# A Graph and Attention Layer with a Routed Feed-Forward Net on One Core: Token Search, Placing and the Net's First Lists Rewritten

## The chip, the cores and the metric

The kernel runs on one core of a Trainium2 chip. The metric is the device time of one execution in microseconds, start to end. The profile is one execution, and all its times are counted from the start of its span. The engines are named as the profile names them: PE is TensorE, DVE VectorE, ACT ScalarE, POOL GpSimd, SP SyncE.

## The reference

The input is 12,500 rows of 256 floats with 200,000 edges sorted by destination. Three things are added up, and a routed net follows:

```
xn = layernorm(x)
x = x + graph(xn) + attention_block(xn)
#   graph: relu(mean over edges of xn[src] @ W_l.T + b_l + xn @ W_r.T) + xn
#   attention_block: linear attention with elu+1, its norm, an MLP, its norm, residual
x = x + routed(layernorm(x))

def routed(x):                          # 12500 rows
    weights = x @ wr + br               # one number per row
    _, idx = top_k(weights, 6250)
    sel = idx[:6249]                    # KK = 6249 rows
    y = gelu(x[sel] @ w1 + b1) @ w2 + b2    # 256 -> 1024 -> 256
    y = y * weights[sel]
    return zeros.at[sel].set(y) + x
```

The change concerns how the 6249 rows are chosen and brought to the routed net. The graph and attention stages compute the same with the same instructions.

## The kernel before, in words

Rows are held as 98 blocks (NBLK) of 128; row number = block x 128 + lane. A [128, 98] tile has one entry per row of the input. The work runs in stages, and each engine has one instruction list, written out by hand, with semaphores between the engines; an engine does its list in order, so the order in the source is the order in time. `own.link(x)` makes the engine that issued x wait until x is done before its next instruction.

1. Layer norm, gathers of source rows (POOL, L708), one-hot segment sums on PE, attention and MLP. None of it is changed.
2. **The graph product stage**: 49 steps of two blocks. POOL loads `lin_raw` (L722), PE turns the means (L1535) and multiplies (L1718, L1722), DVE adds and takes statistics (L1076 to L1102), ACT scales (L1440), SP stores rows to `out_rows` (L636). Ahead of it DVE's list has the reciprocals of the counts (L1058), the sum of `wr` (L1059) and the small tables of the search (L1061 to L1069). Its first job in the stage itself is L1076, which waits for PE's first product.
3. **The search** (DVE L1128 to L1181, PE L1736 to L1743). DVE makes a sortable integer of each row's weight, splits it into two halves of 16 bits held as float32, and finds the KK-th largest in eight rounds of one digit of four bits, four rounds for the high half and four for the low one. In a round DVE compares all 98 entries with 15 candidates (L1152, in two parts of 4 and 3 chunks of 14 blocks: 840 and 630 results per lane, the candidate running fastest in the result `s_ge`, float16). PE sums each of the seven chunks over lanes into PSUM by a product with a tile of ones (L1741), DVE adds over blocks (L1159), counts the candidates that still have KK rows (L1161) and forms the next candidates (L1164, L1166). Behind the first comparisons of all DVE also writes the coefficients of the layer norm for the net (L1139 to L1142), which SP stores to `coef_d` (L653).
4. **The ranks** (DVE L1180 to L1202, PE L1745 to L1756): ties, and for every chosen row its place in the list of 6249, as a column (0 to 48) and a lane.
5. **The placing** (DVE L1203 to L1213, ACT L1466 to L1470, PE L1757 to L1763): for each of seven chunks of 14 blocks DVE compares the columns (`s_is`, 14 x 49 results, L1207) and the lanes (`s_oh`, 14 x 128, L1209) and multiplies `s_is` by the block number (`s_pc`'s second half, L1212); ACT multiplies `s_is` by the lane (`s_pc`'s first half, L1470). PE then takes 14 products of `s_oh` (the weights) with `s_pc` (L1761). Two buffers of each alternate; from the third chunk on DVE and ACT wait until PE is done with the chunk two before. All arrays are float16 with the entry 0..48 or 0..127 running fastest.
6. **The net** (25 steps of up to 256 rows). DVE writes the row lists (L1217 to L1220). POOL copies a step's list (L731) and issues two gathers of rows (L743) and two of coefficients (L746), step by step. Float32 products are made of rounded parts and what is left: ACT rounds the weights (L1474, L1475), DVE subtracts (`fw1_l` L1224, `fw2_l` L1225), norms a step's rows (L1237), PE turns them (L1774), ACT rounds them (L1481), DVE subtracts (L1231), and PE multiplies (L1782), 48 matmuls with `w1` and 48 with `w2` in a step. PE waits once, ahead of the first step, until both subtractions of the weights are done (`f_wl`).

The two loops around which the change is made are these:

```
for h in range(2):                                        # L1149
    o, w = PCH * sum(CHALF[:h]), PCH * CHALF[h]
    v.tensor_tensor(s_ge[:, o:o + w, :], keys[:, o:o + w].unsqueeze(2)...,   # float32
                    bcast(s_cand, w, CAND), ALU.is_ge).then_inc(s_cnt, 1)
...
e.wait_ge(f_wh, 2)                                        # L1223
v.tensor_tensor(fw1_l, fw1_s, fw1_h.bitcast(f32), ALU.subtract).then_inc(f_wl, 1)
v.tensor_tensor(fw2_l, fw2_s, fw2_h.bitcast(f32), ALU.subtract).then_inc(f_wl, 1)
```

Of the kernel before, what the change touches and what calls it, by code (L numbers as in the profile page):

```python
# [13 lines left out]
P = 128  # L14
# [26 lines left out]
HALFD = 16 // DIGIT  # L41
NDIG = 2 * HALFD
# [3 lines left out]
CHALF = (NPCH - NPCH // 2, NPCH // 2)  # L46
# [69 lines left out]
def build(nc, x, src, dst, W_l, b_l, W_r, Wq, Wk, Wv, Wm, W1, W2, g1, b1, g2, b2, wr, br, w1, fb1, w2, fb2, out):  # L116
# [13 lines left out]
    with ctx:  # L130
# [221 lines left out]
        f_in = [sem(f"f_in{i}") for i in range(FSLOTS)]  # L352
        f_T_ps = sem("f_T_ps")
# [68 lines left out]
        s_tab = part(topk, 0, (HALFD, 16))[:, :, 0:CAND]  # L422
        s_unit = part(topk, 64, (HALFD, 16))[:, :, 0:CAND]
        s_cand, s_next, s_counts, s_got = (topk[:, a:a + CAND] for a in (128, 144, 160, 176))
        s_found, s_prefix, s_left, s_above = (topk[:, a:a + 1] for a in (192, 193, 194, 195))
        s_key, s_half = (topk[:, a:a + NBLK].bitcast(i32) for a in (300, 400))
        s_hi, s_low, s_over, s_keys = (topk[:, a:a + NBLK] for a in (500, 600, 700, 800))
# [3 lines left out]
        iota16, tri16, ones16 = (topk16[:, a:a + P] for a in (0, 128, 256))  # L431
        col16, blk16 = topk16[:, 384:384 + NSEL], topk16[:, 448:448 + NBLK]
# [4 lines left out]
        s_ge = work[:, 6144:6144 + NBLK * CAND // 2].bitcast(f16).rearrange("p (b k) -> p b k", k=CAND)  # L437
        s_oh, s_is, s_pc = ([work[:, a + w * k:a + w * k + PCH * m // 2].bitcast(f16).rearrange("p (b m) -> p b m", b=PCH)
# [220 lines left out]
        def _(e):  # L659
# [73 lines left out]
            def f_io(i, s, j):  # L733
# [8 lines left out]
                for u in range(n):  # L742
# [22 lines left out]
        def _(e):  # L765
# [302 lines left out]
            v.tensor_scalar(col16, iotaf[:, 0:NSEL], -64.0, None, ALU.add)  # L1068
# [65 lines left out]
            own.link(v.tensor_copy(s_hi, s_half))
            v.tensor_copy(s_low, s_key)

            def coefficients():

                v.tensor_copy(gcoef[:, :, 0], gmv[:, :, 0])  # L1139
                v.tensor_copy(gcoef[:, :, 2], wtok[:, :])  # L1140
                own.link(v.reciprocal(gve, gg))
                v.tensor_tensor(gcoef[:, :, 1], gf, gve, ALU.mult).then_inc(coef_set, 1)  # L1142

            def search(keys, first):

                v.memset(s_prefix, 0.0)
                own.link(v.tensor_copy(s_cand, s_tab[:, 0, :]))
                for r in range(HALFD):
                    n = first + r  # L1149
                    for h in range(2):  # L1150
                        o, w = PCH * sum(CHALF[:h]), PCH * CHALF[h]
                        v.tensor_tensor(s_ge[:, o:o + w, :], keys[:, o:o + w].unsqueeze(2).to_broadcast([P, w, CAND]),  # L1152
                                        bcast(s_cand, w, CAND), ALU.is_ge).then_inc(s_cnt, 1)
                    if r + 1 < HALFD:
                        v.tensor_scalar(s_next, s_tab[:, r + 1, :], s_prefix, None, ALU.add)
                    if n == 0:
                        coefficients()
                    e.wait_ge(s_tot, n + 1)
                    own.link(v.tensor_reduce(s_counts, part(ps[:, BA, :], 0, (PCH, CAND)).rearrange("p b k -> p k b"),  # L1159
                                             AX.X, ALU.add))  # L1160
                    own.link(v.tensor_scalar(s_got, s_counts, float(KK), None, ALU.is_ge, ALU.add,  # L1161
                                             accum_out=s_found))
                    if r + 1 < HALFD:
                        own.link(v.scalar_tensor_tensor(out=s_cand, in0=s_unit[:, r, :], scalar=s_found, in1=s_next,  # L1164
                                                        op0=ALU.mult, op1=ALU.add))
                    own.link(v.scalar_tensor_tensor(out=s_prefix, in0=s_unit[:, r, 0:1], scalar=s_found, in1=s_prefix,  # L1166
                                                    op0=ALU.mult, op1=ALU.add))
# [337 lines left out]
        def _(e):  # L1505
# [281 lines left out]
            def f_body(i, s, j):  # L1787
# [16 lines left out]
                if past(i, 1):  # L1804
                    e.wait_ge(f_yb, i)
# [35 lines left out]
```

## Time and profile before

| What | us |
|---|---|
| Median of 3 runs (2602.32 to 2604.92) | 2603.88 |
| The profiled execution's own time | 2605.66 |
| Its span, first to last instruction | 2603.9 |
| PE busy in the span | 2193.5 (84%) |
| DVE busy in the span | 1329.9 (51%) |
| POOL busy in the span | 1695.5 (65%) |
| PE's mean granted clock, as a share of 2.4 GHz | 0.934 |

Of a row of the profile: `L1209 DVE TENSOR_TENSOR work<-srcI 128x1792 f16` is an instruction of line 1209 on DVE which writes the tile `work` from `srcI`, 128 lanes of 1792 results. In a timeline, a row begins with the start and the duration in us; brackets hold the time that the engine stood idle before it and what ended that. In a table by stage, each engine has its busy time and its number of instructions. Durations of DVE instructions include a start and an end that overlap the neighbour, so that two which follow each other with no wait start closer together than the first one's duration.

### The profile page before, as it was taken

How to read it: one execution, taken by the hardware profiler on the slowest of the kernel's cores; microseconds unless marked ns; L12 is line 12 of the kernel's file. 1: busy time of each engine (PE TensorE's matmuls, PEld its weight loads, DVE VectorE, ACT ScalarE, POOL GpSimd, SP SyncE). 2: the span in 40 equal slices, each digit the busy share in tenths (PEclk: the TensorE clock that was granted, in tenths of full speed). 3: DMA queues.
4: the chain of work that ended last, by engine and by line, in shares of the span. 5: the costliest groups of instructions: out<-in, count | busy, mean ns of one | idle time of the engine just before them, and what ended most of it. 6: DMA issues, size and time to landing. Idle time of an engine off the chain costs nothing.

```text
span 2603.9 us, 48868 instructions
## 1 busy us (share of the span) xinstructions
PE 2193.5 (84%) x13352; PEld 1818.9 (70%) x13353; DVE 1329.9 (51%) x3157; ACT 901.4 (35%) x1949; POOL 1695.5 (65%) x1817
## 2 busy tenths in 40 slices
PE   1399999997888888888888888988899799379998
PEld 0287777775667666666676666777677688279998
DVE  8644444443444344454444454455555599844444
ACT  8433333331222222222222222222222268344554
POOL 3577777777777777777777777777777411045553
PEclk7699999998898999999999999999999899589999
DMA  9766666654555555555555555555555489611111
GB/s 326 232 194 186 184 184 179 188 181 146 160 157 153 152 154 164 157 160 155 153 158 160 153 161 157 152 153 165 158 162 166 142 276 297 214 34 43 45 44 35
DMA packets 218373, 419.29 MB, mean 161 GB/s; under 512 B 40580, under 2 KB 107142, under 8 KB 218287
## 3 DMA queue, kind: packets, MB, share of 16 engines
q0 software_dynamic: 88352, 243.57, 33.0%
q1 hardware_dynamic: 129118, 173.95, 19.9%
q8 instruction: 34, 0.56, 0.1%
q10 hardware_dynamic: 816, 0.79, 0.1%
q14 instruction: 53, 0.43, 0.1%
HBM read 321.63 MB, written 96.52 MB: 161 GB/s over the span
## 4 chain that ended last, share of the span: by engine, by line
PE 45%; POOL 29%; issue 13%; DVE 7%; DMA 5%; ACT 1%; DVEq 1%; POOLq 0%; ACTq 0%
POOL gath_raw L708 28%; PE ps L1782 11%; PE ps L1629 6%; PE ps L1550 5%; PE ps L1552 4%; PE ps L1595 4%; DMA gath_raw<-xtab,srcI 3%; PE ps L1722 3%; PE ps L1639 3%; PE ps L1535 2%; PE ps L1677 2%; PE ps L1647 1%; DVE stats L784 1%; PE ps L1609 1%; DVE gath_raw L803 1%
## 5 line engine op out<-in xcount | busy, mean ns | idle before, releaser
L708 POOL DMA_INDIRECT gath_raw<-xtab,srcI x1563 | 1483.6, 949 | 476.5 <-issue 460.7
L1550 PE MATMUL ps<-gath_raw,onehot 128*128 128x256 f16 x1956 | 480.3, 283 | 202.8 <-DMA gath_raw<-xtab,srcI 107.6
L880 DVE SCALAR_TENSOR_TENSOR onehot<-ps,blkbase,dstF 128x512 f32 x489 | 353.9, 745 | 257.8 <-issue 154.5
L1552 PE MATMUL ps<-gath_raw,onehot 128*128 128x257 f16 x1956 | 481.5, 283 | 0.0
L1550 PEld LDWEIGHTS ps<-gath_raw,onehot 128*128 x1956 | 195.2, 100 | 292.9 <-issue 263.4
L1629 PE MATMUL ps<-work,w_s 128*128 128x256 f32 x1568 | 392.9, 407 | 2.2 <-issue 1.7
L1629 PEld LDWEIGHTS ps<-work,w_s 128*128 128x128 f32 x1568 | 311.7, 204 | 48.7 <-issue 2.7
L954 DVE BATCH_NORM_STATS2 stats<-ps 128x6 f32<-128x256 f32 x196 | 74.4, 421 | 449.2 <-PE ps L1677 444.6
L1782 PE MATMUL ps<-split_raw 128*128 128x256 f32 x2376 | 293.3, 285 | 1.7 <-DVE split_raw L1231 1.5
L1782 PEld LDWEIGHTS ps<-split_raw 128*128 128x128 f32 x2376 | 288.4, 193 | 2.4 <-issue 1.9
L1363 ACT ACTIVATE work<-ps 128x512 f32<-128x512 f32 x98 | 58.5, 597 | 496.8 <-PE ps L1629 496.8
L1552 PEld LDWEIGHTS ps<-gath_raw,onehot 128*128 x1956 | 197.2, 101 | 40.3
L1595 PE MATMUL ps<-wkv_s,work 128*128 128x256 f32 x784 | 183.1, 387 | 5.4 <-issue 4.7
L1639 PE MATMUL ps<-w_s,work 128*128 128x256 f32 x784 | 182.3, 385 | 0.0
L1595 PEld LDWEIGHTS ps<-wkv_s,work 128*128 128x128 f32 x784 | 146.1, 191 | 25.3 <-issue 5.4
L1639 PEld LDWEIGHTS ps<-w_s,work 128*128 128x128 f32 x784 | 144.9, 190 | 18.5
L1398 ACT ACTIVATE work<-ps,b_s,g_s 128x256 f32<-128x256 f32 x98 | 49.9, 560 | 247.3 <-PE ps L1535 247.3
L1368 ACT ACTIVATE small<-small 128x2 f32<-128x2 f32 x98 | 19.9, 203 | 329.6 <-DVE small L962 329.6
L1495 ACT ACTIVATE agg<-ps,fb_s 128x256 f32<-128x256 f32 x200 | 83.9, 470 | 138.4 <-PE ps L1782 138.4
L1535 PE MATMUL ps<-ident,work 128*128 128x128 f32 x784 | 124.6, 282 | 5.6 <-ACT work L1422 5.6
L722 POOL DMA_DIRECT2D lin_raw<-lin_d x49 | 26.0, 532 | 124.6 <-PE ps L1722 109.0
L1535 PEld LDWEIGHTS ps<-ident,work 128*128 128x128 f32 x784 | 91.1, 142 | 17.8 <-ACT work L1422 5.7
(223 smaller groups left out, 2989.9 us busy)
## 6 DMA issues: line engine op xcount, KB each, us to landing
work<-x_in SPq DMA_DIRECT2D x98, 256.0 KB, 3.2
lin_raw<-lin_d POOLq DMA_DIRECT2D x49, 512.0 KB, 4.4
gath_raw<-xtab,srcI POOLq DMA_INDIRECT x1563
agg<-x_in SPq DMA_DIRECT2D x14, 896.0 KB, 7.4
xt_d<-work SPq DMA_DIRECT2D x49, 256.0 KB
q_d<-work SPq DMA_DIRECT2D x49, 256.0 KB, 2.7
work<-q_d SPq DMA_DIRECT2D x49, 256.0 KB, 3.4
work<-xt_d SPq DMA_DIRECT2D x49, 256.0 KB, 3.1
```

Source lines behind the costliest of these rows:

```text
L708: e.indirect_dma_start(out=gath[:, TPG * s + t, 0:2 * D], out_offset=None, in_=xtab[:, :], in_offset=bass.IndirectOffsetOnAxis(ap=srcI[:, ...
L880: v.scalar_tensor_tensor(out=onehots[:, ds(p % OHN * TPG, TPG), :], in0=ps[:, columns:columns + 1, 0:P].to_broadcast(shape), scalar=blkbas ...
L954: last = v.bn_stats(ln_st[k][:, u, :], src[:, u, :])
L1495: last = a.activation(fh[:, c, :], bank(BB + h)[:, c % 2, :], ACT.Gelu_apprx_tanh, bias=fb1_s[:, c:c + 1])
L1535: last = t.transpose(bank(b)[:, c, u * P:(u + 1) * P], of[:, u, c * P:(c + 1) * P], ident[:, :])
L1550: t.matmul(ps[:, ds(BG + k % 2, 1), 0:D], oh, gath[:, r, 0:D], start=False, stop=False, skip_group_check=True)
L1552: last = t.matmul(ps[:, ds(BG + k % 2, 1), 0:AGW], oh, gath[:, r, D:2 * D + 1], start=False, stop=q == TPG - 1, skip_group_check=True)
L1595: last = t.matmul(bank(BC + b)[:, u, :], kxT[s][:, c, u * P:(u + 1) * P], wkv_s[:, c, b * D:(b + 1) * D], start=c == 0, stop=c == 1)
L1629: last = t.matmul(bank(BD + h)[:, o_ % 2, :], w1_s[:, c, o_ * P:(o_ + 1) * P], (mxT[s] if c < 2 else mynT)[:, c % 2, :], start=c == 0, sto ...
L1639: last = t.matmul(bank(BF)[:, u, :], mh1[:, c, u * P:(u + 1) * P], w2_s[:, c, :], start=c == 0, stop=c == 3)
L1722: last = t.matmul(to[:, u, :], gaT[i % 2][:, c, u * P:(u + 1) * P], wlT[:, c, :], start=False, stop=c == 1, skip_group_check=True)
L1782: last = t.matmul(to, left[l], right[r], start=start and k == 0, stop=stop and k == 2)
```

## The change

- **Digits as tokens.** Eight digits of four bits are read straight from the 32-bit key (a shift and a mask into `s_nib`, then a cast with 1 added), each kept as float16 1 to 16. One search of eight rounds replaces two of four. The fixed candidates 2 to 16 stand in a table laid out over blocks (`cand_rep`), and instead of new candidates each round ends with a new token: the next digit where the entry is equal to what was found, 32 where it is above, 0 where below (three DVE operations).
- **Layout.** `s_ge`, `s_oh`, `s_is` and `s_pc` are transposed inside a lane: the block runs fastest, and the candidate, the lane or the column is the slower one. The constants they are compared with are spread into tables beforehand (`cand_rep` 15 x 98, `lane_rep` 128 x 14, `col_rep` 49 x 14), in the space of the gathered rows, behind a wait for the last group. Everything compared is float16. PE's weights and moving data of L1761 are then columns with a step of 14 elements (28 bytes); in the search its moving data are 15 runs of 14.
- **Halves.** The first comparison of a round covers 3 chunks, the second 4 (it was 4 and 3).
- **Coefficients.** The four instructions behind the first round are spread over the first four rounds.
- **The net's start.** POOL signals `f_sent` when it has issued the gathers of step 0; DVE waits for that before it subtracts `fw1_l`, and subtracts `fw2_l` behind step 0's own norm and subtraction. PE waits for `fw1_l` ahead of step 0's first product and for `fw2_l` ahead of its second.

```diff
-CHALF = (NPCH - NPCH // 2, NPCH // 2)
+CHALF = (NPCH // 2, NPCH - NPCH // 2)
...
+        s_dig = [topk16[:, 1920 + 112 * r:1920 + 112 * r + NBLK] for r in range(NDIG)]
+        rep16 = gath_raw[:, 0:2048].bitcast(f16)
+        cand_rep = part(rep16, 0, (CAND, NBLK))
+        lane_rep = part(rep16, 1472, (P, PCH))
+        col_rep = part(rep16, 3264, (NSEL, PCH))
...
-        s_ge = work[:, 6144:6144 + NBLK * CAND // 2].bitcast(f16).rearrange("p (b k) -> p b k", k=CAND)
+        s_ge = work[:, 6144:6144 + NBLK * CAND // 2].bitcast(f16).rearrange("p (k b) -> p k b", k=CAND)
...
+                if not past(i, 1):
+                    e.sem_inc(f_sent, 1)
...
-            for r in range(HALFD):
-                step = float(1 << (16 - DIGIT * (r + 1)))
-                v.tensor_scalar(s_tab[:, r, :], iotaf[:, 1:CAND + 1], step, None, ALU.mult)
-                v.memset(s_unit[:, r, :], step)
-            v.tensor_copy(iota16, iotaf[:, :])
+            e.wait_ge(grp_used, NG)
+            v.tensor_copy(cand_rep, spread(iotaf[:, 2:CAND + 2], CAND, NBLK))
+            v.tensor_copy(lane_rep, spread(iotaf[:, 0:P], P, PCH))
+            v.tensor_scalar(col_rep, spread(iotaf[:, 0:NSEL], NSEL, PCH), -64.0, None, ALU.add)
+            v.memset(s_counts[:, CAND:CAND + 1], 3.0e38)
...
+            def digit(r):
+                own.link(v.tensor_scalar(s_nib, s_key, 32 - DIGIT * (r + 1), CAND, ALU.logical_shift_right, ALU.bitwise_and))
+                own.link(v.tensor_scalar(s_dig[r], s_nib, 1.0, None, ALU.add))
+            digit(0)
+            token = s_dig[0]
+            for r in range(NDIG):
+                for h in range(2):
+                    b = slice(PCH * sum(CHALF[:h]), PCH * sum(CHALF[:h + 1]))
+                    v.tensor_tensor(s_ge[:, :, b], over(token[:, b], CAND), cand_rep[:, :, b], ALU.is_ge).then_inc(s_cnt, 1)
+                if r + 1 < NDIG:
+                    digit(r + 1)
...
+                if r == 2:
+                    own.link(v.reciprocal(gve, gg))
...
+                e.wait_ge(s_tot, r + 1)
+                own.link(v.tensor_reduce(s_counts[:, 0:CAND], part(ps[:, BA, :], 0, (CAND, PCH)), AX.X, ALU.add))
+                own.link(v.tensor_scalar(s_got, s_counts, float(KK), None, ALU.is_ge, ALU.add, accum_out=s_found))
+                if r + 1 < NDIG:
+                    v.scalar_tensor_tensor(out=s_among, in0=token, scalar=s_found, in1=s_dig[r + 1],
+                                           op0=ALU.is_equal, op1=ALU.mult)
+                    own.link(v.tensor_scalar(s_above_at, token, s_found, 2.0 * (CAND + 1), ALU.is_gt, ALU.mult))
+                    token = s_next[r % 2]
+                    own.link(v.tensor_tensor(token, s_among, s_above_at, ALU.add))
...
+                v.tensor_tensor(s_is[k], col_rep, over(s_col[:, b], NSEL), ALU.is_equal).then_inc(s_in_col, 1)
+                v.tensor_tensor(s_oh[k], lane_rep, over(s_pos[:, b], P), ALU.is_equal)
...
+                v.tensor_tensor(s_pc[k][:, NSEL:2 * NSEL, :], s_is[k], over(blk16[:, b], NSEL), ALU.mult).then_inc(s_a, 1)
...
-            e.wait_ge(f_wh, 2)
+            e.wait_ge(f_sent, 1)
+            e.wait_ge(f_wh, 1)
             v.tensor_tensor(fw1_l, fw1_s, fw1_h.bitcast(f32), ALU.subtract).then_inc(f_wl, 1)
-            v.tensor_tensor(fw2_l, fw2_s, fw2_h.bitcast(f32), ALU.subtract).then_inc(f_wl, 1)
...
             f_norm(0, 0, 0)
             f_low_x(0, 0)
+            e.wait_ge(f_wh, 2)
+            v.tensor_tensor(fw2_l, fw2_s, fw2_h.bitcast(f32), ALU.subtract).then_inc(f_wl, 1)
...
-                    last = t.matmul(ps[:, BD, 0:2 * NSEL], s_oh[c % 2][:, k, :], s_pc[c % 2][:, k, :],
+                    last = t.matmul(ps[:, BD, 0:2 * NSEL], s_oh[c % 2][:, :, k], s_pc[c % 2][:, :, k],
...
-            e.wait_ge(f_wl, 2)
+            e.wait_ge(f_wl, 1)
...
+                else:
+                    e.wait_ge(f_wl, 2)
```

## Rows read from the trace of the kernel before

**Rows 1.** The page's shares by engine and line of the chain that ended last

```profile
PE 45%; POOL 29%; issue 13%; DVE 7%; DMA 5%; ACT 1%; DVEq 1%; POOLq 0%; ACTq 0%
```

**Rows 2.** Stages: window, length, busy us (PE, PEld, DVE, ACT, POOL), clock, DMA share, GB/s

```profile
2220.50:2253.10 32.60, 11.42 (x56) 5.73 (x56) 26.26 (x79) 15.80 (x33) 0.00 (x0) 0.50 1.01 341
2258.00:2284.00 26.00, 9.28 (x98) 7.77 (x98) 24.60 (x21) 9.38 (x9) 0.00 (x0) 0.50 0.00 1
2298.80:2603.90 305.10, 297.73 (x2470) 297.18 (x2470) 139.44 (x245) 154.55 (x325) 145.97 (x163) 0.99 0.14 42
```

**Rows 3.** Groups by shape, DVE: count, busy us, mean ns, idle before

```profile
L1119 DVE TENSOR_TENSOR gath_raw<-gath_raw 128x98 f32<-128x98 f32 x1 | 0.3, 261 | 0.0
L1193 DVE TENSOR_TENSOR srcI<-srcI 128x98 f16<-128x98 f16 x1 | 0.2, 211 | 0.0
```

**Rows 4.** Timeline of one round of the search (the second), to the next round's first row

```profile
2226.42 1.76 DVE L1152 TENSOR_TENSOR work<-dstF 128x840 f16<-128x840 f32 x2
2228.23 0.31 PEld L1741 LDWEIGHTS ps<-work,srcI 128*128 128x128 f16 x3 [0.25 <-DVE work L1152]
2228.97 0.38 DVE L1159 TENSOR_REDUCE dstF<-ps 128x15 f32<-128x210 f32 x1 [0.66 <-PE ps L1741]
2229.60 0.23 DVE L1164 SCALAR_TENSOR_TENSOR dstF<-dstF 128x15 f32<-128x15 f32 x1
2230.12 1.76 DVE L1152 TENSOR_TENSOR work<-dstF 128x840 f16<-128x840 f32 x2
```

**Rows 5.** Timeline, DVE: where the search begins and ends, and three operations in it

```profile
2220.52 0.21 DVE L1128 TENSOR_SCALAR dstF<-wtok 128x98 f32<-128x98 f32 x1
2221.31 0.21 DVE L1132 TENSOR_SCALAR dstF<-dstF 128x98 int32<-128x98 int32 x1
2224.31 0.76 DVE L1141 RECIPROCAL gath_raw<-gath_raw 128x98 f32<-128x98 f32 x1
2237.70 0.32 DVE L1173 SCALAR_TENSOR_TENSOR dstF<-dstF 128x98 f32<-128x98 f32 x1
2253.12 0.32 DVE L1180 TENSOR_SCALAR_CACHE_REDUCE srcI<-dstF 128x98 f16<-128x98 f32 x1
```

**Rows 6.** Timeline of the placing's last chunk and what follows it

```profile
2279.02 0.86 DVE L1207 TENSOR_TENSOR work<-srcI 128x686 f16<-128x686 f16 x1
2279.80 2.02 DVE L1209 TENSOR_TENSOR work<-srcI 128x1792 f16<-128x1792 f16 x1
2281.74 0.86 DVE L1212 TENSOR_TENSOR work<-work,srcI 128x686 f16<-128x686 f16 x1
2282.66 1.32 PE L1761 MATMUL ps<-work 128*128 128x98 f16 x14 [2.17 <-DVE work L1212]
2284.02 0.21 DVE L1217 TENSOR_SCALAR dstF<-ps 128x49 f32<-128x49 f32 x1 [1.42 <-PE ps L1761]
```

**Rows 7.** Timeline from the row lists to the net's first products

```profile
2284.74 2.28 DVE L1224 TENSOR_TENSOR split_raw<-agg,split_raw 128x2048 fp32r<-128x2048 f32 x1
2284.89 2.18 POOL L731 COPY agg<-agg 128x4 int32<-128x4 int32 x1 [78.17 <-DVE agg L1220]
2287.91 2.25 POOL L743 DMA_INDIRECT agg<-out_rows,agg  x1 [0.83 <-POOL agg L731]
2293.00 0.94 POOL L746 DMA_INDIRECT agg<-coef_d,agg  x1 [0.30 <-issue]
2293.94 0.20 POOL L731 COPY agg<-agg 128x4 int32<-128x4 int32 x1
2294.96 0.96 POOL L743 DMA_INDIRECT agg<-out_rows,agg  x1 [0.81 <-POOL agg L731]
2295.35 0.73 DVE L1237 TENSOR_SCALAR agg<-agg 128x256 f32<-128x256 f32 x2 [6.12 <-DMA agg<-coef_d,agg]
2298.82 8.04 PE L1782 MATMUL ps<-split_raw 128*128 128x256 f32 x48 [1.50 <-DVE split_raw L1231]
```

**Rows 8.** Timeline, DVE: the first addition of the graph product stage

```profile
2085.48 0.69 DVE L1076 SCALAR_TENSOR_TENSOR agg<-ps,work 128x512 f32<-128x512 f32 x1 [5.91 <-PE ps L1722]
```

More of the change, by code:

```diff
@@ L421, in build @@
         topk = dstF[:, :, :].rearrange("p g t -> p (g t)")
[L422 to L427, printed above, removed]
+        s_counts, s_got = (topk[:, a:a + CAND + 1] for a in (160, 176))
+        s_found, s_left, s_above = (topk[:, a:a + 1] for a in (192, 194, 195))
+        s_key, s_sign, s_nib = (topk[:, a:a + NBLK].bitcast(i32) for a in (300, 400, 500))
+        s_bits = topk[:, 800:800 + NBLK]
         s_rk, s_rcol, s_rpos = (topk[:, a:a + NBLK].bitcast(i32) for a in (900, 1000, 1100))
@@ L1134, in _ @@
[L1134 to L1167, printed above, removed]
@@ L1177, in _ @@
-            search(s_keys, HALFD)
-            v.tensor_scalar(s_gt, s_keys, s_prefix, None, ALU.is_gt, ALU.add, accum_out=s_above)
-            v.tensor_scalar(s_eq, s_keys, s_prefix, None, ALU.is_equal).then_inc(s_cnt, 1)
+            own.link(v.tensor_scalar(s_bits, wtok[:, :], 0.0, None, ALU.add))
+            bits = s_bits.bitcast(i32)
+            own.link(v.tensor_scalar(s_sign, bits, 31, -(1 << 31), ALU.arith_shift_right, ALU.bitwise_or))
+            own.link(v.tensor_tensor(s_key, bits, s_sign, ALU.bitwise_xor))
@@ new lines, in digit, with over @@
+            def digit(r):
+                own.link(v.tensor_scalar(s_nib, s_key, 32 - DIGIT * (r + 1), CAND, ALU.logical_shift_right, ALU.bitwise_and))
+                own.link(v.tensor_scalar(s_dig[r], s_nib, 1.0, None, ALU.add))
+            def over(ap, n):
+                return ap.unsqueeze(1).to_broadcast([P, n, ap.shape[1]])
+            digit(0)
[6 more added lines that the diff above has]
+                    digit(r + 1)
+                if r == 0:
+                    v.tensor_copy(gcoef[:, :, 0], gmv[:, :, 0])
+                if r == 1:
+                    v.tensor_copy(gcoef[:, :, 2], wtok[:, :])
+                if r == 2:
+                    own.link(v.reciprocal(gve, gg))
+                if r == 3:
+                    v.tensor_tensor(gcoef[:, :, 1], gf, gve, ALU.mult).then_inc(coef_set, 1)
+                e.wait_ge(s_tot, r + 1)
[7 more added lines that the diff above has]
+                    own.link(v.tensor_tensor(token, s_among, s_above_at, ALU.add))
@@ L1183, in ranked @@
+            v.tensor_scalar(s_gt, token, s_found, None, ALU.is_gt, ALU.add, accum_out=s_above)
+            v.tensor_scalar(s_eq, token, s_found, None, ALU.is_equal).then_inc(s_cnt, 1)
             def ranked(n):
@@ L1469, in _ @@
                     e.wait_ge(s_mm, c - 1)
-                a.activation(s_pc[c % 2][:, :, 0:NSEL], s_is[c % 2], ACT.Copy, scale=pcol[:, 0:1]).then_inc(s_lane, 1)
+                a.activation(s_pc[c % 2][:, 0:NSEL, :], s_is[c % 2], ACT.Copy, scale=pcol[:, 0:1]).then_inc(s_lane, 1)
             e.wait_ge(ffw_in, 32)
@@ L1740, in _ @@
                         e.wait_ge(s_cnt, 2 * r + 1 + (c > 0))
-                    last = t.matmul(ps[:, BA, 0:PCH * CAND], ones16, flat(s_ge[:, c * PCH:(c + 1) * PCH, :]),
+                    last = t.matmul(part(ps[:, BA, :], 0, (CAND, PCH)), ones16, s_ge[:, :, c * PCH:(c + 1) * PCH],
                                     start=c == 0, stop=c == NPCH - 1)
```

34 lines of the change are left out of this document (9 added, 25 removed).

## The prediction

> **What bounds the kernel now.** I read the page's chain first: PE holds 45% of it, POOL 29% and DVE only 7% [rows 1]. So DVE looks like a side matter, and over the whole span it is. The table by stage says where it is not. For 32.60 us of the search DVE is busy 26.26, and for 26.00 us of the placing it is busy 24.60, while PE has 11.42 and 9.28 and sits at half its clock (0.50, 1.2 GHz). Behind them lies the net, where PE is busy 297.73 of 305.10 us: whatever is saved ahead of it moves the net forward whole [rows 2]. The third place is the gap between the row lists and the net's first product, in which POOL's issues are the chain [rows 7]. These three stretches, some 73 us, are all that the change can win from.
>
> **Comparing at float16, block fastest (the large term).** The comparisons of the placing run at one result per cycle of 0.96 GHz: starts are 0.78 us apart for 686 results, 1.94 for 1792, 0.78 for the multiplication, 3.50 a chunk [rows 6]. That is 1.0417 ns a result and 0.066 us an instruction. Their data are float16 already, but one operand repeats the same element along the fastest direction. What would they cost with both operands running? One pair of rows of equal length answers: 98 results took 261 ns in float32 and 211 ns in float16 with all three operands plain [rows 3]. The 50 ns between them are 98 x 0.52 ns, half a cycle each. So I take 0.5208 ns a result. A chunk becomes (686 + 1792 + 686) x 0.5208 ns + 3 x 0.066 = 1.65 + 0.20 = 1.85 us. Seven chunks save 7 x (3.50 - 1.85) = **11.6 us**. ACT's product of a chunk starts behind the first comparison; even if all of ACT's 9.38 us in the placing [rows 2] were these seven, one would be 1.34, less than the 1.43 that DVE's other two then take.
>
> PE's side of a chunk is 1.32 us for 14 matmuls [rows 6], at half clock. It fits in 1.85 as long as a matmul stays under 1.85 / 14 = 0.13 us. After the change weights and moving data are read with a step of 28 bytes, and no row shows a matmul reading so. From below the cost is nothing (98 columns at 1.2 GHz are 0.082 us, 14 of them 1.14 of the 1.32, so there is no gain to be had); from above nothing in the trace bounds it, and I carry it as a rival. I take none, because the half clock leaves every column twice the time it has at full clock.
>
> The Trainium skill speaks against this (SBUF — State Buffer, section Door 1: The DMA port swizzle, on cachelines): SBUF has lines of 16 bytes, and a read that goes to a new line each time pays a penalty, so that float16 may be stepped by 8 elements for free, and the change steps by 14. The page gives no price; by its rule PE could need twice the time, and the sum would be that of the first rival below. No row of this trace shows it.
>
> **The search.** A round is now 3.70 us [rows 4]. Step by step:
> - The two comparisons, 1470 results: 1.76 becomes 630 x 0.5208 + 0.066 for the first and 840 x 0.5208 + 0.154 (start and end) for the second, 0.985 us.
> - From their end to the reduction: PE's last group took 2228.97 - 2228.18 = 0.79 with three matmuls. It now has four, each 210 columns at 1.2 GHz, 0.175: 0.965.
> - Reduction and count: 2229.60 - 2228.97 = 0.63, unchanged.
> - The new candidates took 0.52 (2229.60 to 2230.12). The token takes three operations: a SCALAR_TENSOR_TENSOR of 98 (0.32 long, 0.24 to the next start, since nothing waits) [rows 5], a waited-for TENSOR_SCALAR (0.25 and 0.035) and a TENSOR_TENSOR (0.21 and 0.035) [rows 3]: 0.77.
>
> A round is 3.35, the last 2.58 without the token. The next digit's two waited-for operations (0.25 each) lie in PE's 0.97 us, as does a copy in rounds 0 and 1. In round 2 the reciprocal of 0.76 [rows 5] comes on top: 0.5 + 0.8 exceeds the cover by some 0.25 us. Ahead of the rounds five waited-for operations take the place of eight: three of them span 0.79 (2220.52 to 2221.31) [rows 5], five 1.28. Between the halves nothing is left. In all 1.28 + 7 x 3.35 + 0.25 + 2.58 = 27.56 us, against 2253.12 - 2220.52 = 32.60 [rows 5]: **5.0 us**. Its parts: comparisons 8 x 0.775 = 6.2 saved, PE's fourth matmul 8 x 0.175 = 1.4 given back, the token 7 x 0.25 = 1.75 given back, ends and middle 2.0 saved.
>
> **The net's start.** Both subtractions begin beside POOL's first copy, each 2.28 us. The copy took 2.18 us where the next one took 0.20, and the first gather 2.25 where a later one took 0.96 [rows 7]; nothing else differs, so the subtractions hold POOL up. Without them POOL's last issue of step 0 ends 1.98 + 1.3 = 3.3 us earlier, 5.8 us behind the lists instead of 9.1, and its data would reach DVE at 7.2 (L746's start to L1237 is 2.35) instead of 10.5. But DVE now begins `fw1_l` at 5.8 and ends it at 8.15, and L1237 is behind it in DVE's list. What is late next is thus the subtraction: **2.35 us** saved, 3.3 the bound if it cost nothing, and 1.4 if POOL's next copy or gather gets ahead of it. Who else waits: POOL's issues for step 1 are held up by `fw1_l` and perhaps by `fw2_l` (2 x 2.2 us), so step 1's rows are there at about 17.5 us behind the lists; PE asks for them when its first 48 matmuls, 8.04 us long [rows 7], are over, at 11.6 + 8.0 = 19.6. `fw2_l` ends at 14, far ahead of that. Cost nothing, slack 2 us.
>
> **The tables.** `cand_rep`, `lane_rep`, `col_rep` are 3948 results, 4.1 us at one per cycle, some 3.2 us more than what they replace. DVE stands idle 5.91 us before L1076 [rows 8]: hidden even at one per cycle. Without that cover it would be 3.2 us. The wait for the last group is over by then. **Transfers**: the lists are now due near 2268; the DMA share is 0.00 from 2258.00 on [rows 2], so stores, weights and coefficients have landed.
>
> **The sum** is 5.0 + 11.6 + 2.35 = 19.0 us. The profiled execution took 2605.66 us (span 2603.9), so it would take 2586.7. The median of the runs, 2603.88, is 1.8 below it: **2584.9 us**.
>
> **The rivals.**
> 1. PE's stepped reads bind the placing, mildly: each matmul twice 0.082. A chunk is 14 x 0.163 = 2.3 us; the placing is 7 x 0.45 = 3.1 us longer and the last chunk's tail 1.1. That gives 2589.1, still faster. For it: no row shows such a read. Chance 0.12.
> 2. The new comparisons don't run at two per cycle (a repeated outer direction or runs of 14 spoil it). Then the placing saves nothing, the search is 6.2 - 5.0 = 1.2 us longer than now, the lists save 2.35: 2602.7, no change. For it: the one float16 row is a single plain run of 98 [rows 3]. Against: the fastest direction is now as in that row, and runs of 15 cost nothing extra at one per cycle (1470 results in 1.76) [rows 4]. Chance 0.08.
> 3. Slower: stepped reads at a price that makes PE the bound of the placing. It decides from where 98 matmuls outlast what is saved: to lose 0.2% (5.2 us), the placing must take 26.0 + 5.0 + 2.35 + 5.2 = 38.6 us instead of 26.0, less 2.0 at its ends 36.6, or 0.37 us a matmul, 4.6 times now. At six times (0.49) it is 98 x 0.49 + 2 = 50 us, and the time 2603.9 + 24 - 7.35 = 2620.6. Against: no row shows a matmul that slow. Chance 0.04.
> 4. The lists' gain fails (POOL's next issue gets ahead of `fw1_l`, step 1 late): 1 to 3 us back, 2587. It is inside the range. Chance 0.06.
>
> **The numbers.** The forecast has 0.70. What two runs of this kernel can be told apart by is 0.2%, 5.2 us. Faster takes the forecast, rivals 1 and 4: 0.88; no change is rival 2, 0.08; slower is rival 3, 0.04. Downward the range adds the lists' bound of 3.3 instead of 2.35 (0.95), a cheaper token and a run's scatter of 1.3: 2581.5. Upward it takes in rivals 1 and 4: 2591.
>
> **What would show it.** In the profile after: L1209's successor near 1.08 us for 1792 results and chunks 1.85 us apart, with PE's 14 matmuls still 1.3; rounds 3.35 us apart; POOL's first copy 0.2 us; the first net product about 11.6 us behind the row lists instead of 14. Wrong would be: 2.0 us for 1792 results (rival 2); DVE idle before a chunk's first comparison, ended by PE (rivals 1, 3); the first addition of the graph product stage later than now.

## The result, and the profile after

| | before | after |
|---|---|---|
| Median of six runs, us | 2604.4 | 2592.99 |
| Ratio, 95% interval | | 0.9955 (0.9941 to 0.9968) |
| Span of the profiled execution, us | 2603.9 | 2589.7 |
| Search, first key operation to L1180 / L1178 | 32.6 | 28.0 |
| Ranks | 4.9 | 4.9 |
| Placing, first comparison to the row lists' first operation | 26.0 | 20.0 |
| End of the row lists to the net's first product | 14.0 | 12.85 |
| First product to the end | 305.1 | 304.9 |

The kernel became 11.4 us faster, with the interval 8.3 to 15.4 (0.0032 to 0.0059 of 2604.4). Forecast were 19.0, and the measured time lies 2.0 us above the range. One of the six executions of the changed kernel was slow, 5558.56 us; the ratio leaves it out, and without it the median would be 2592.84. The three stretches give 4.6 + 6.0 + 1.15 = 11.75 us, so the trace accounts for the measured gain. The two profiled spans differ by 14.2, but 2.3 of these lie ahead of the search, where none of the three terms of the forecast lies: its first operation starts at 2218.25 instead of 2220.52.

The table by stage of the changed kernel, beside [rows 2] (window, length, busy time of PE, PEld, DVE, ACT and POOL with counts, granted clock, DMA share, GB/s):

```profile
2218.20:2246.30 28.10, 11.22 (x56) 5.89 (x56) 22.38 (x86) 15.84 (x33) 0.00 (x0) 0.50 1.02 345
2251.10:2271.20 20.10, 18.01 (x98) 13.84 (x98) 13.56 (x22) 9.68 (x9) 0.00 (x0) 0.50 0.00 1
2284.80:2589.70 304.90, 297.44 (x2470) 296.90 (x2470) 141.53 (x246) 154.67 (x325) 147.53 (x163) 0.99 0.14 42
```

The second row is where the expected gain went. In the placing DVE's busy time fell from 24.60 us to 13.56, as meant, but PE's rose from 9.28 to 18.01 of 20.10 us, on the same 98 products at the same clock. The stage has a new bound.

A chunk of the placing, as a timeline (start, duration; in brackets the idle time before and what ended it), beside [rows 6]:

```profile
2253.13 18.01 PE L1758 MATMUL ps<-work 128*128 128x98 f16 x98 [3.06 <-DVE work L1208]
2263.54 0.52 DVE L1205 TENSOR_TENSOR work<-gath_raw,srcI 128x686 f16<-128x686 f16 x1 [0.60 <-PE ps L1758]
2263.97 1.09 DVE L1206 TENSOR_TENSOR work<-gath_raw,srcI 128x1792 f16<-128x1792 f16 x1
2264.97 0.51 DVE L1208 TENSOR_TENSOR work<-work,srcI 128x686 f16<-128x686 f16 x1
2266.08 0.52 DVE L1205 TENSOR_TENSOR work<-gath_raw,srcI 128x686 f16<-128x686 f16 x1 [0.60 <-PE ps L1758]
2271.17 0.21 DVE L1212 TENSOR_SCALAR dstF<-ps 128x49 f32<-128x49 f32 x1 [3.14 <-PE ps L1758]
```

The comparisons run at two results per cycle: 1792 in 1.08 to 1.09 us where it was 2.02, 686 in 0.52 where it was 0.86. But PE, once started, has one unbroken run of 98 matmuls, and DVE stands 0.60 us ahead of a chunk until PE gives a buffer back. Chunks start 2266.08 - 2263.54 = 2.54 us apart, not 1.85. And the last chunk ends with 3.14 us of waiting where it was 1.42. This is what the prediction named as the sign of rival 1.

A round of the search, beside [rows 4]:

```profile
2233.31 0.99 DVE L1156 TENSOR_TENSOR work<-srcI,gath_raw 128x630 f16<-128x630 f16 x2
2233.85 1.41 PE L1738 MATMUL ps<-work,srcI 128*128 128x210 f16 x7 [1.97 <-DVE work L1156]
2234.46 0.21 DVE L1146 TENSOR_SCALAR srcI<-dstF 128x98 f16<-128x98 int32 x1
2235.36 0.38 DVE L1168 TENSOR_REDUCE dstF<-ps 128x15 f32<-128x210 f32 x1 [0.69 <-PE ps L1738]
2235.99 0.32 DVE L1171 SCALAR_TENSOR_TENSOR srcI<-srcI,dstF 128x98 f16<-128x98 f16 x1
2236.75 0.99 DVE L1156 TENSOR_TENSOR work<-srcI,gath_raw 128x630 f16<-128x630 f16 x2
```

The comparisons take 0.99, the token 2236.75 - 2235.99 = 0.76, and the next digit's operations (L1146 is the second) are hidden beside PE. Only PE's part is longer than worked out: 1.06 us from the end of the comparisons to the reduction, not 0.965. A round is 3.44. PE's seven matmuls are one run of 1.41 us, where it was 1.43: moving data in runs of 14 elements cost PE nothing here.

The start of the net, beside [rows 7]; the row lists end at 2271.99 (L1215, 2271.78 and 0.21 long):

```profile
2272.05 0.19 POOL L736 COPY agg<-agg 128x4 int32<-128x4 int32 x1 [67.67 <-DVE agg L1215]
2273.06 1.05 POOL L748 DMA_INDIRECT agg<-out_rows,agg  x1 [0.83 <-POOL agg L736]
2274.28 2.29 DVE L1220 TENSOR_TENSOR split_raw<-agg,split_raw 128x2048 fp32r<-128x2048 f32 x1 [2.30 <-POOLq L755]
2274.42 3.02 POOL L751 DMA_INDIRECT agg<-coef_d,agg  x1 [0.30 <-issue]
...
2281.37 0.73 DVE L1232 TENSOR_SCALAR agg<-agg 128x256 f32<-128x256 f32 x2 [4.79 <-DMA agg<-coef_d,agg]
2284.84 7.68 PE L1779 MATMUL ps<-split_raw 128*128 128x256 f32 x48 [1.50 <-DVE split_raw L1226]
```

The copy is short now (0.19, it was 2.18), but the stall has only moved: the second gather takes 3.02 us, where the third and fourth take 0.95 and 0.94. The subtraction was let go at 2274.28 by "POOLq L755", the queue's signal written behind all four gathers, when one of the four had run. The norm (L1232) still waits for its data, 4.79 us after the subtraction.

The tables, made ahead of the graph product stage (DVE's timeline), beside [rows 8]:

```profile
2077.36 1.67 DVE L1073 CAST gath_raw<-iotaf 128x1470 f16<-128x1470 f32 x1
2078.94 1.08 DVE L1074 CAST gath_raw<-iotaf 128x1792 f16<-128x1792 f32 x1
2079.94 0.86 DVE L1075 TENSOR_SCALAR gath_raw<-iotaf 128x686 f16<-128x686 f32 x1
2084.31 0.69 DVE L1086 SCALAR_TENSOR_TENSOR agg<-ps,work 128x512 f32<-128x512 f32 x1 [3.10 <-PE ps L1719]
```

Of 5.91 us of idle time 3.10 are left: the tables are hidden, as forecast.

### The profile page after: what moved, and what is told of

It is laid out like the page before. It is cut to its first block, busy times and chain, and to the rows that moved or that the text cites. A ratio compares the mean times of both kernels' runs of the same rounds, so it can differ in the third digit from the quotient of the medians.

```text
span 2589.7 us, 48874 instructions
## 1 busy us (share of the span) xinstructions
PE 2200.0 (85%) x13352; PEld 1826.8 (71%) x13353; DVE 1316.4 (51%) x3156; ACT 902.0 (35%) x1949; POOL 1696.3 (66%) x1817
## 4 chain that ended last, share of the span: by engine, by line
POOL 37%; PE 37%; issue 14%; DVE 5%; DMA 4%; ACT 1%; DVEq 1%; POOLq 0%; SPq 0%; ACTq 0%
POOL gath_raw L713 37%; PE ps L1779 11%; PE ps L1626 4%; PE ps L1547 3%; PE ps L1719 3%; PE ps L1549 3%; PE ps L1592 3%; DMA gath_raw<-xtab,srcI 3%; PE ps L1636 2%; PE ps L1532 2%; DVE stats L791 1%; PE ps L1674 1%; PE ps L1644 1%; DVE gath_raw L810 1%; PE ps L1715 1%
```

## The experiments

The chips of these runs were slower than the first one: the kernel before took 3063.6 us (median of 25 runs) beside the first four, 3109.2 beside the next four (one run) and 3095.9 (18 runs) beside the last four. Nearly all of that lies ahead of the search: in the changed kernel run again (e11), the first addition of the graph product stage comes at 2568.7 us instead of 2084.3, which is 484 of the 495 us by which its span is longer. The search took 28.0 us in every one of these runs and the placing 20.0 wherever it was unchanged, as on the first chip. Repeats of one kernel scatter by 8 to 24 us there, so the verdicts below rest on the stretches, each read from one profile; the ratios are given beside them. The next four, e5 to e8, ran once each, 3091.1, 3094.2, 3101.4 and 3078.5 us beside 3109.2, and no verdict rests on these times: e6, whose placing is 8 us longer than before the change, would come out 15 us faster.

**e1: the placing undone.**

```diff
-                v.tensor_tensor(s_oh[k], lane_rep, over(s_pos[:, b], P), ALU.is_equal)
+                v.tensor_tensor(s_oh[k], bcast(iota16, PCH, P), s_pos[:, b].unsqueeze(2).to_broadcast([P, PCH, P]),
+                                ALU.is_equal)
...
-                    last = t.matmul(ps[:, BD, 0:2 * NSEL], s_oh[c % 2][:, :, k], s_pc[c % 2][:, :, k],
+                    last = t.matmul(ps[:, BD, 0:2 * NSEL], s_oh[c % 2][:, k, :], s_pc[c % 2][:, k, :],
...
```

The comparison of the columns and both products are turned back in the same way.

> The changed kernel with the placing as it was before (entry running fastest, comparisons at one result per cycle). Theory A (the stepped reads make PE the bound of the placing, so the new layout saves 6.0 us there and not 11.6): the placing takes 26.0 us again instead of 20.0, a chunk 3.50, PE's 14 matmuls 1.32 us a chunk; time 2593.0 + 6.0 = 2599.0. Theory B (the layout gave its 11.6 and the loss lies outside the three stretches): 2604.6.

Placing 26.0 us, as in theory A. The ratio to the kernel before, 0.9990 (0.9972 to 1.0008), holds theory A's time (0.9979) and theory B's (1.0001), so it is the stretch that decides. PE's matmuls, by the view of one line (minimum, median and maximum ns), are back at their old length:

```profile
L1761 PE MATMUL ps<-work x98: 260/282/285, 2705.5 to 2727.6; 128*128 128x98 f16 x98
```

**e2: the net's start undone.**

```diff
-            e.wait_ge(f_sent, 1)
-            e.wait_ge(f_wh, 1)
+            e.wait_ge(f_wh, 2)
             v.tensor_tensor(fw1_l, fw1_s, fw1_h.bitcast(f32), ALU.subtract).then_inc(f_wl, 1)
+            v.tensor_tensor(fw2_l, fw2_s, fw2_h.bitcast(f32), ALU.subtract).then_inc(f_wl, 1)
...
```

The signal, the later `fw2_l` and PE's two separate waits go too.

> The changed kernel with both subtractions of the net's weights ahead of the first lists again. Theory A (the signal leaves POOL too early, so that part is worth 1.15 us and not 2.35): from the last instruction of the row lists to the net's first product 14.0 us instead of 12.85; time 2594.2. Theory B (that part gave its 2.35): 2595.4, the difference in the stretch 2.35. Theory C (it gave nothing): 2593.0 and the stretch unchanged.

From the start of the lists' last instruction to the first product: 14.2 us, against 13.1 in the changed kernel on these chips (e7, e11) and 13.0 on the first. That is 1.1 to 1.2, theory A (whose 14.0 and 12.85 count from that instruction's end, 0.2 later). The same stretch is 13.0 to 13.4 in the versions that change the placing alone (e1, e5, e6, e8), so it is good to some 0.3 us: enough against B's 2.35 and C's nothing. The ratio, 0.9974 (0.9962 to 0.9985), doesn't tell the theories apart: their times are 0.9956 to 0.9965.

**e3: the search alone.** The edits of e1 and e2 together.

> Only the search of the change, with the placing and the net's start of before. Theory A (the search is worth what its stretch shows, 4.6 us, and the parts add up): 2604.4 - 4.6 = 2599.8, search 28.0 us, placing 26.0, row lists to first product 14.0. Theory B (the parts don't add up, what is saved in one is given back in the next): over 2602.

Search 28.0, placing 26.0, and 14.5 us from the start of the lists' last instruction to the first product (14.2 in the kernel before and in e2). The ratio, 0.9991 (0.9970 to 1.0012), holds both theories' times (0.9982 and over 0.9991). Each part is thus seen to be independent of the others by its stretch; that the whole time adds up was not resolved.

**e4: wait for POOL's copy instead of the signal.**

```diff
-                if not past(i, 1):
-                    e.sem_inc(f_sent, 1)
...
-            e.wait_ge(f_sent, 1)
+            e.wait_ge(fstage[1], 1)
```

> The changed kernel in which DVE waits, ahead of its first subtraction, for POOL's copy of the second step's list instead of the signal that POOL's instruction list raises behind the four gathers of the first. Theory A (the signal is raised when the gathers are queued, not when they have run; a copy runs in POOL's own order behind them): the subtraction starts about 6.0 us behind the row lists instead of 2.3, no gather of the first step is longer than 1.1 us, the first product comes 11.7 us behind the row lists instead of 12.85; time 2591.8. Theory B (the second gather is long for another reason): a gather of 3 us remains, and the subtraction starts later on top: 14 us or more, time 2594 or more.

The timeline behind the row lists, which end at 2724.53 (L1212, 2724.32 and 0.21 long):

```profile
2725.61 1.05 POOL L747 DMA_INDIRECT agg<-out_rows,agg  x1 [0.83 <-POOL agg L735]
2726.96 0.99 POOL L750 DMA_INDIRECT agg<-coef_d,agg  x1 [0.30 <-issue]
...
2730.46 0.19 POOL L735 COPY agg<-agg 128x4 int32<-128x4 int32 x1
2730.69 2.29 DVE L1217 TENSOR_TENSOR split_raw<-agg,split_raw 128x2048 fp32r<-128x2048 f32 x1 [6.16 <-POOL agg L735]
2732.90 0.73 DVE L1229 TENSOR_SCALAR agg<-agg 128x256 f32<-128x256 f32 x2
2736.36 7.39 PE L1776 MATMUL ps<-split_raw 128*128 128x256 f32 x48 [1.50 <-DVE split_raw L1223]
```

All four gathers of the first step are at 1.05 us or less (the two left out took 0.95 each), the subtraction starts 6.16 behind the lists, the first product 11.83 (forecast 11.7). Theory A holds. The stall has moved on to a gather of the second step (L747, 2731.47, 2.35 us), which is in no hurry. The norm (L1229) now begins the moment the subtraction ends, with no wait for its data: the subtraction is what is late, as the prediction had it. The ratio, 0.9961 (0.9943 to 0.9978), holds both theories' times (0.9952, and 0.9960 or more).

**e5: weights contiguous, moving data stepped.**

```diff
-                    last = t.matmul(ps[:, BD, 0:2 * NSEL], s_oh[c % 2][:, :, k], s_pc[c % 2][:, :, k],
+                    last = t.matmul(ps[:, BD, 0:2 * NSEL], s_oh[c % 2][:, k, :], s_pc[c % 2][:, :, k],
...
```

DVE's comparison of the lanes is again that of e1, so that `s_oh` is written with the lane running fastest.

> The changed kernel with the lanes' comparison and its result, PE's weights in the placing, laid out as before (contiguous), and the moving data still read with a step of 14 elements. DVE's chunk is then 0.43 + 1.94 + 0.43 = 2.80 us. Theory M (the moving data's step costs): PE's 14 matmuls of a chunk still take about 2.5 us, 0.18 each. Theory W (the weights' step costs): they take 1.32 us, 0.082 apart. Theory C (neither; DVE's and PE's traffic in one memory collide): about 2.5 us only while DVE writes. Placing about 22.5 us by M, 21.1 by W.

The first 28 matmuls of the placing, the line's view, and the last 14 matmuls:

```profile
2747.61 5.43 PE L1760 MATMUL ps<-work 128*128 128x98 f16 x28 [4.00 <-DVE work L1210]
L1760 PE MATMUL ps<-work x98: 336/356/359, 2747.6 to 2766.8; 128*128 128x98 f16 x98
2764.46 2.64 PE L1760 MATMUL ps<-work 128*128 128x98 f16 x14 [0.19 <-DVE work L1210]
```

A matmul still lasts 356 ns, where it was 282 before the change, and 28 take 5.43 us. The placing takes 22.4 us. Theory M. Theory C falls too: DVE's last write of the placing (L1210, 2763.90) ends at 2764.41, and the 14 matmuls behind it still take 2.64 us.

**e6: moving data contiguous, weights stepped.**

```diff
-                    last = t.matmul(ps[:, BD, 0:2 * NSEL], s_oh[c % 2][:, :, k], s_pc[c % 2][:, :, k],
+                    last = t.matmul(ps[:, BD, 0:2 * NSEL], s_oh[c % 2][:, :, k], s_pcb[c % 2][:, k, :],
...
```

`s_pcb` is `s_pc`'s space with the entry running fastest; DVE and ACT write it through a stepped view.

> The changed kernel with PE's moving data in the placing laid out as before (contiguous; DVE and ACT write them with a step), and the weights still read with a step of 14 elements. DVE's chunk is 0.43 + 1.00 + 0.78 = 2.21 us. Theory M (the moving data's step costs): PE's 14 matmuls of a chunk take 1.32 us, DVE is the bound, placing 7 x 2.21 + 1.4 = 16.9 us. Theory W (the weights' step costs): 14 matmuls stay at 2.5 us, placing 20 us.

```profile
2741.51 1.36 PE L1760 MATMUL ps<-work 128*128 128x98 f16 x14 [5.99 <-DVE work L1210]
2741.83 3.58 ACT L1469 ACTIVATE work<-work,pcol 128x686 f16<-128x686 f16 x1 [1.11 <-DVE work L1207]
2742.72 3.39 DVE L1210 TENSOR_TENSOR work<-work,srcI 128x686 f16<-128x686 f16 x1
```

PE's 14 matmuls take 1.36 us with stepped weights: theory M again, now from the other side (and DVE's L1208 writes from 2741.72 on beside them, which is against theory C once more). The placing, forecast at 16.9, took 34.2 us, for a reason neither theory had: writing 686 float16 results with a step of 98 elements takes DVE 3.39 us and ACT 3.58, where the same counts took 0.86 and 0.88 in the kernel before. The two overlap in every chunk, so what one of them takes alone was not seen.

**e7: a table of steps.** Nine groups of 16 matmuls at the end of PE's list, whose results nothing reads; the fourth is this:

```diff
+            for q in range(16):
+                t.matmul(ps[:, BG, 0:98], mb_w[:, 0:128:1], mb_m[:, 0:777:8], start=True, stop=True)
...
```

> The changed kernel, with nine groups of 16 float16 matmuls (128 weights columns, 98 moving columns) added at the end of PE's list, steps of weights and moving data in elements: (1,1) (1,2) (1,4) (1,8) (1,14) (2,1) (8,1) (14,1) (14,14). PE's clock is full there. Theory M: the weights' step changes nothing; the moving data's step of 8 and 14 makes a matmul longer, steps of 1 and 2 do not. If the price is one more cycle a column, it is 98 / 2.4 = 41 ns more a matmul at full clock (half of what the placing shows at half clock); if it is a fixed time of memory, it is about 80 to 100 ns more at either clock. Theory W: only the groups with a weights' step of 8 or 14 are longer.

The line's view of the nine groups in order, from (1,1) to (14,14), where the first number is the step of the weights and the second that of the moving data:

```profile
L1818 PE MATMUL ps<-work x16: 207/207/218, 3083.9 to 3084.6; 128*128 128x98 f16 x16
L1820 PE MATMUL ps<-work x16: 205/208/209, 3084.6 to 3085.3; 128*128 128x98 f16 x16
L1822 PE MATMUL ps<-work x16: 250/269/269, 3085.4 to 3086.7; 128*128 128x98 f16 x16
L1824 PE MATMUL ps<-work x16: 352/353/353, 3086.8 to 3089.4; 128*128 128x98 f16 x16
L1826 PE MATMUL ps<-work x16: 355/357/359, 3089.6 to 3092.2; 128*128 128x98 f16 x16
L1828 PE MATMUL ps<-work x16: 265/282/285, 3092.4 to 3093.6; 128*128 128x98 f16 x16
L1830 PE MATMUL ps<-work x16: 282/284/285, 3093.7 to 3094.9; 128*128 128x98 f16 x16
L1832 PE MATMUL ps<-work x16: 282/284/285, 3095.0 to 3096.2; 128*128 128x98 f16 x16
L1834 PE MATMUL ps<-work x16: 356/361/363, 3096.3 to 3099.0; 128*128 128x98 f16 x16
```

And windows in the fourth group, in the fifth (two), in the sixth and in the ninth (PE busy, granted clock, DMA share, GB/s):

```profile
3086.80:3089.40 2.60, 2.60 (x17) 1.00 0.16 48
3089.40:3090.00 0.60, 0.60 (x6) 1.00 0.00 0
3091.20:3091.80 0.60, 0.60 (x5) 0.50 0.00 0
3092.40:3093.60 1.20, 1.20 (x17) 0.50 0.00 0
3098.00:3098.60 0.60, 0.60 (x5) 1.00 0.00 0
```

From first to last start, over 15 intervals: a matmul every 0.04 to 0.05 us at moving steps 1 and 2, about 0.09 at step 4, and 0.17 to 0.18 at steps 8 and 14. Steps 1 to 8 ran at the full clock (2.4 GHz). In the group of step 14 the clock fell from 1.00 to 0.50, and its matmuls last 355 to 359 ns all the same; the placing of the changed kernel, all at half clock, had (18.01 - 0.36) / 97 = 0.182. So the price of a column at step 14 is a time and not a number of PE's cycles: about 1.8 ns at either clock. At the full clock it is the same 1.8 ns at step 8 (16 bytes) and 0.9 at step 4 (8 bytes); neither was run at half clock. DVE and ACT are idle beside the fourth to ninth groups (busy 0.00 from 3086.80 on), so nothing that they write is the cause.

Theory M holds, but neither of its two forms of the price does. The added time is not the same at either clock, as the second form had it: it is 0.13 us at the full clock (0.175 against 0.045) and 0.10 at half (0.182 against 0.082). What is the same is the time of the whole read. Stepped weights at half clock cost nothing (0.08 apart at steps 2, 8 and 14). What they cost at full clock with contiguous moving data stays open; beside moving data of step 14 they add nothing that shows (ninth group, 0.18, at 1.00 in its later part).

**e8: pairs of blocks.** Two blocks run fastest, then the lane or column, then the pair; PE's step is 2 elements.

```diff
+            def table(t):
+                return t.unsqueeze(1).to_broadcast([P, PCH // 2, t.shape[1], 2])
+            def pair_of(v_, m):
+                return v_.rearrange("p (b t) -> p b t", t=2).unsqueeze(2).to_broadcast([P, PCH // 2, m, 2])
-                v.tensor_tensor(s_oh[k], lane_rep, over(s_pos[:, b], P), ALU.is_equal)
+                v.tensor_tensor(s_oh[k], table(lane_rep), pair_of(s_pos[:, b], P), ALU.is_equal)
...
-                    last = t.matmul(ps[:, BD, 0:2 * NSEL], s_oh[c % 2][:, :, k], s_pc[c % 2][:, :, k],
+                    last = t.matmul(ps[:, BD, 0:2 * NSEL], s_oh[c % 2][:, k // 2, :, k % 2], s_pc[c % 2][:, k // 2, :, k % 2],
...
```

The columns' comparison and both products have the same layout.

> The changed kernel with the placing's arrays laid out by pairs of blocks: two blocks run fastest, then the lane or column, then the seven pairs. PE then reads with a step of 2 elements (4 bytes). Theory A (DVE needs only two neighbouring elements for its rate of two per cycle, and PE reads a step of 2 at full rate): chunks 1.85 us apart, 14 matmuls 1.32 us, placing 7 x 1.85 + 1.4 = 14.4 us. Theory B (DVE's rate falls with runs of two): 3.5 us a chunk, placing 26 us. Theory C (PE's matmuls are slow at any step but 1): 0.16 to 0.18 us each, placing 18 to 20 us.

```profile
2743.54 1.08 DVE L1213 TENSOR_TENSOR work<-gath_raw,srcI 128x1792 f16<-128x1792 f16 x1
2743.25 1.32 PE L1765 MATMUL ps<-work 128*128 128x98 f16 x14 [0.53 <-DVE work L1215]
2745.11 1.32 PE L1765 MATMUL ps<-work 128*128 128x98 f16 x14 [0.53 <-DVE work L1215]
```

The placing takes 14.5 us (forecast 14.4): DVE keeps two results per cycle with runs of two (1792 in 1.08), PE is at 1.32 a chunk, chunks are 1.86 apart, and PE waits for DVE again. Theory A. This is the prediction's own sum for the placing, with the stepped read taken out.

**The changed kernel and three versions on one chip.** e11 is the changed kernel without an edit. Then come the timed e8, e9, which is e8 with e4's edit, and e10, which is e8 without a signal and with the first subtraction moved behind the norm. The last edit, shown against e9:

```diff
-            e.wait_ge(fstage[1], 1)
-            e.wait_ge(f_wh, 1)
-            v.tensor_tensor(fw1_l, fw1_s, fw1_h.bitcast(f32), ALU.subtract).then_inc(f_wl, 1)
...
             f_norm(0, 0, 0)
+            e.wait_ge(f_wh, 1)
+            v.tensor_tensor(fw1_l, fw1_s, fw1_h.bitcast(f32), ALU.subtract).then_inc(f_wl, 1)
             f_low_x(0, 0)
```

> The changed kernel itself, on the chip of the next three, so that they can be set against it. Search 28.0 us, placing 20.0, row lists to first product 12.85; 11.4 us less than the kernel before, if the chip's first stages scatter little enough to show it.

> The layout by pairs, timed. Its placing took 14.5 us, 11.5 less than before the change. Theory (PE's stepped read was the missing 5.5 us of that part and nothing takes its place): 5.5 us less than the changed kernel, 17 less than the kernel before. Rival (DVE's and POOL's earlier start at the net meets the transfers of the coefficients or the last stores): row lists to first product over 13.5 us, part of the 5.5 lost.

> The layout by pairs, and DVE waits for POOL's copy of the second list instead of the signal. Theory: both gains add, placing 14.5 us, row lists to first product 11.8 us; 6.5 us less than the changed kernel, 18 less than the kernel before. Rival (the net's steps take the second gain back, since the second step's lists are later): the stretch from the first product to the end is 1 us longer than with pairs alone.

> The layout by pairs, no signal, and DVE subtracts the first weights behind its norm of the first step's rows (which waits for the gathers anyway) and ahead of that step's own subtraction. Theory: the norm is no longer behind a subtraction of 2.3 us, which now lies beside PE's transposes and ACT's rounding for 1.8 of it; first product 11.3 us behind the row lists, 0.5 less than with the copy; 7 us less than the changed kernel. Rival (what is late next is the subtraction again, and PE waits for it): 11.8 us or more.

| | median us | ratio to before | placing | lists' end to first product | first product to end |
|---|---|---|---|---|---|
| before | 3095.9 | | | | |
| e11, changed | 3089.3 | 0.9972 (0.9957 to 0.9988) | 20.0 | 12.9 | 311.6 |
| e8, pairs | 3084.8 | 0.9956 (0.9937 to 0.9975) | 14.5 | 12.8 | 306.9 |
| e9, pairs and copy | 3077.9 | 0.9948 (0.9929 to 0.9966) | 14.5 | 11.8 | 309.1 |
| e10, pairs, behind the norm | 3081.4 | 0.9954 (0.9926 to 0.9982) | 14.5 | 11.0 | 310.0 |

The placing and the start of the net went as worked out, e10's start even better than the 11.3 expected. e8's rival, over 13.5 us at the net's start, fell (12.8). The timeline of e10, whose lists end at 2752.88 (L1219, 2752.67 and 0.21 long):

```profile
2760.18 0.73 DVE L1233 TENSOR_SCALAR agg<-agg 128x256 f32<-128x256 f32 x2 [7.30 <-DMA agg<-coef_d,agg]
2760.83 2.28 DVE L1239 TENSOR_TENSOR split_raw<-agg,split_raw 128x2048 fp32r<-128x2048 f32 x1
2763.86 3.07 PE L1782 MATMUL ps<-split_raw 128*128 128x256 f32 x13 [1.71 <-DVE split_raw L1227]
```

The norm waits for its data alone, 7.30 us, the 7.2 that the prediction had as the time of arrival. All three versions have a lower median than the changed kernel, but the intervals overlap. The stretch from the first product to the end lies between 306.9 and 311.6 in these four profiles, longest in the changed kernel, and these 5 us are more than e9 and e10 could gain at the net's start. Shown are the stretches: 5.5 us in the placing and 1.1 to 1.9 at the start. That the whole time falls by as much was not resolved on this chip. e9's rival, that the net gives the second gain back, stays open: 309.1 against e8's 306.9 is on its side, and within that scatter.

## Why the prediction was wrong

**PE in the placing: the step that failed.** The prediction had DVE's side right: two results per cycle from one pair of rows 50 ns apart, and 1.85 us for its part of a chunk (0.43 + 1.00 + 0.43 by the starts after). It failed where it took no cost for PE's stepped reads, "because the half clock leaves every column twice the time it has at full clock". Half clock leaves 0.83 ns a column; the read took 1.8 (e7, and 0.182 us for 98 in the placing), so the slower clock hides less than half of it. The limit up to which a matmul fits, 0.13 us, was worked out rightly, and 0.182 is over it. The placing gained 6.0 us and not 11.6, 5.6 less. That was rival 1, given 0.12. It counted the price as exactly twice the contiguous read, 0.163, and its 3.1 + 1.1 = 4.2 us are 1.4 too few. e5 and e6 show that it is the moving data's step and not the weights', and e8 that with the step gone the placing is 14.5 us, against the 14.4 of the prediction's sum.

The warning that the prediction cites stands confirmed in its direction (the Trainium skill, SBUF — State Buffer, section Door 1: The DMA port swizzle): a float16 read stepped beyond 16 bytes pays. By its figure a step of up to 8 elements would be free; e7 has a step of 4 at twice the time of a step of 1, and 8 at four times, at the full clock. Here the measurement decides.

**The signal in the net's start: the second step that failed.** "But DVE now begins `fw1_l` at 5.8": the subtraction was taken to begin when the four gathers had been issued. It began 2.3 us behind the lists. The signal, which stands behind the four gathers in POOL's list, was raised when one of them had run, and the next gather took 3.02 us. e4 has the same edit with a signal that an operation of POOL's raises in its own order: the subtraction begins at 6.16, no gather of the first step is stretched, and the first product comes at 11.83 us, near the 11.6 that the prediction's steps lead to. The mechanism (a subtraction on DVE holds POOL's copy or gather up, and what is late next is the subtraction itself) was right; where the signal is raised was wrong. Rival 4 named the loss but put its cause at step 1's copy.

**The search: right, a term too small.** 4.6 us against 5.0. The comparisons (0.99 against 0.985) and the token (0.76 against 0.77) were met; PE's part was 0.04 to 0.10 us a round longer. Its seven matmuls are one run (1.41 us, started 0.54 behind the round's start) and end 1.95 behind it, where the step had the reduction begin already (0.985 + 0.965). In the second, fourth and last round the reduction follows some 0.04 us later, in the fifth to seventh 0.10; why it differs stays open.

**The tables and the rest: right.** The tables are hidden, with 3.10 us to spare. No transfer was late: the lists' first operation was let go by PE (L1212, 3.14), and the net behind the first product took 304.9 us instead of 305.1.

Put together, 19.0 less 5.6, 1.2 and 0.4 is 11.8, and 11.4 were measured. The loss of rival 1 and one of rival 4's size came together, which the range, made of one at a time, did not hold; added to the forecast, 4.2 + 1.2 give 2590.3, still inside, and what rival 1 had too small (1.4), the search (0.4) and the median before (2604.4, not 2603.88) carry it over 2591. Rivals 2 and 3 fell: DVE's rate doubled, and 0.182 is half of the 0.37 us from which the change would have lost.

## What to carry to other kernels

When a layout is turned to please one engine, price the reading by the next engine in time for each element, not in its cycles, and look for a middle layout: here pairs running fastest gave DVE its doubled rate and PE its full one. Where one engine must have run its work before another begins, let the signal hang on an instruction of that engine in its own order, not on its queue. And in a sum of several parts, let the range hold two misses at once.

## What the runs showed of the hardware that was not expected

- Float16 moving data of a 98-column matmul at full clock: step 1 or 2, a matmul every 0.04 to 0.05 us; step 4, 0.09; step 8, 0.17. At step 14 it is 0.17 to 0.18, whether the clock is full or half. Moving data in runs of 14 elements (the search) cost nothing at half clock, and neither does a step of the weights.
- In e7 PE was busy without a gap, and yet its clock fell from full to half: 1.00 in the group of step 8 (3086.80 to 3089.40) and at the start of that of step 14, 0.50 from the middle of the latter on (3091.20 to 3091.80). It rose again within the ninth group, whose moving data have a step of 14 too (1.00 in 3098.00 to 3098.60).
- Writing float16 with a step of 98 elements takes DVE 3.39 us and ACT 3.58 for 686 results, about 5 ns each, the two at the same time. Which part of the step makes it so was not tried.
- The cast of 15 x 98 results took 1.67 us and that of 128 x 14 took 1.08: one and two results per cycle, with the same source and types. The third table, 49 x 14 (with an addition), took 0.86 for 686, one per cycle. The outer counts are odd in the two slow ones and even in the fast one, and the run of 14 is common to a slow and the fast one; it was not tested.
